# A fused attention and mixture-of-experts kernel: the first expert weight's split moved from the setup into four batches, and the setup's loads and TensorE products put in another order

## The reference

```python
x = x + conv(_ln_c(x))                 # x: 8 x 16 x 16 x 256, "conv" is axial attention
t = _to_tokens(x)                      # 2048 tokens of 256
t = t + ffn(_ln_t(t))                  # 8 experts, one per token, 256 places each

# conv: q, k, v = linear maps of x (256 -> 256)
r_attn = softmax(q . k along a row    - gw * dist(w))
c_attn = softmax(q . k along a column - gw * dist(h))
out = (r_attn v + c_attn v) @ Wo.T + bo

# ffn: logits = x2d @ wg; idx = argmax; a token has a place while its expert has one of 256 free
h  = relu(einsum("ecm,emh->ech", di, w1))     # w1: 8 x 256 x 1024
eo = einsum("ech,ehm->ecm", h, w2)            # w2: 8 x 1024 x 256
out = gate * eo, back at the token's row
```

## Time and profile before

| what | before |
|---|---|
| three executions, us | 206.6, 206.73, 295.39 (median 206.73) |
| span of the profiled execution, first to last instruction, us | 204.0 |
| what lies around the span: median less span, us | 2.7 |
| mean granted TensorE clock in the span | 0.961 |
| PE, DVE, ACT, POOL busy, share of the span | 91%, 72%, 52%, 50% |

### The profile page before, as it was taken

The page is one execution under the profiler, slowest core; times in us unless marked ns, Lnnn a source line. Parts: engine busy times, 40 slices in busy tenths (PEclk is TensorE's granted clock), DMA queues, the critical chain, the costliest instruction groups (busy, mean ns, idle before and its releaser), DMA issues.

```text
span 204.0 us, 4341 instructions
## 1 busy us (share of the span) xinstructions
PE 185.1 (91%) x1404; PEld 176.7 (87%) x1404; DVE 146.6 (72%) x460; ACT 105.4 (52%) x246; POOL 102.8 (50%) x101
## 2 busy tenths in 40 slices
PE   7799399999999985959799999999999999999990
PEld 7699399998798883849789999999999999999980
DVE  0579998898999999776956584866858496465510
ACT  2368367888678644235043927538192653826000
POOL 3327574246456357558400636639183663918351
PEclk9999889999999999676999999999999999999997
DMA  5799750103712211331387639192753909271010
GB/s 186 210 394 346 223 193 0 56 0 72 292 51 83 69 60 53 105 127 51 104 310 240 178 105 345 32 367 79 235 228 113 348 16 345 96 205 42 3 55 33
DMA packets 23294, 30.86 MB, mean 151 GB/s; under 512 B 2559, under 2 KB 20113, under 8 KB 23280
## 3 DMA queue, kind: packets, MB, share of 16 engines
q1 hardware_dynamic: 20704, 25.81, 38.5%
q0 software_dynamic: 1616, 4.02, 5.5%
q10 hardware_dynamic: 960, 0.85, 1.2%
HBM read 22.57 MB, written 8.45 MB: 152 GB/s over the span
## 4 chain that ended last, share of the span: by engine, by line
PE 64%; DVE 22%; issue 5%; DMA 3%; ACT 2%; SPq 1%; POOLq 1%; POOL 1%; DVEq 0%; ACTq 0%
PE banks_v L506 7%; PE banks_v L513 7%; PE banks_v L507 7%; DVE w_low L1143 4%; PE bank_q L513 3%; PE bank_pT L513 3%; PE bank_pT L506 3%; PE bank_pT L507 3%; DMA wg_sb<-in_L_ffn_wg 3%; PE bank_q L506 3%; PE bank_s L513 3%; PE bank_s L506 3%; PE bank_s L507 3%; PE bank_q L507 3%; PE banks_o L580 2%
## 5 line engine op out<-in xcount | busy, mean ns | idle before, releaser
L456 POOL TENSOR_TENSOR w_low<-w_in_sb,w_high 128x1024 fp32r<-128x1024 f32 x16 | 38.4, 2421 | 17.1 <-ACT w_high L826 16.8
L478 POOL DMA_INDIRECT out<-y,goal x16 | 15.7, 979 | 35.5 <-DVE y L1134 29.1
L826 ACT ACTIVATE w_high<-w_in_sb 128x1024 fp32r<-128x1024 f32 x32 | 31.9, 1052 | 1.4 <-DMA w_in_sb<-in_L_ffn_w 1.4
L1143 DVE TENSOR_TENSOR w_low<-w_in_sb,w_high 128x1024 fp32r<-128x1024 f32 x14 | 28.1, 2044 | 4.5 <-ACT w_high L826 4.3
L426 POOL DMA_INDIRECT slots<-row,slot x14 | 14.2, 1016 | 18.1 <-DVE slot L1086 16.1
L870 ACT ACTIVATE h_high<-bank_xT 128x512 fp32r<-128x512 f32 x8 | 4.8, 597 | 28.5 <-PE bank_xT L513 28.5
L644 PE MATMUL bank_xT<-ones_wide 128*128 128x128 f32 x100 | 17.8, 360 | 1.1 <-DVE ones_wide L893 1.1
L580 PE MATMUL banks_o<-v_sb,pT 128*128 128x264 f32 x64 | 18.1, 411 | 0.6 <-DVE logit L1021 0.5
L644 PEld LDWEIGHTS bank_xT<-ones_wide 128*128 128x128 f32 x100 | 17.2, 272 | 1.1 <-DVE ones_wide L893 1.1
L506 PE MATMUL banks_v<-w_high,h_high 128*128 128x256 f32 x64 | 15.9, 287 | 0.0
L507 PE MATMUL banks_v<-w_high,h_low 128*128 128x256 f32 x64 | 15.7, 283 | 0.0
(11 more groups left out here) (200 smaller groups left out, 614.5 us busy)
## 6 DMA issues: line engine op xcount, KB each, us to landing
w_in_sb<-in_L_ffn_w SPq DMA_DIRECT2D x16, 1024.0 KB
slots<-empty SPq DMA_DIRECT2D x1, 2080.0 KB, 13.7
sl<-slots SPq DMA_DIRECT2D x8, 260.0 KB, 3.2
out<-row SPq DMA_DIRECT2D x7, 256.0 KB
sl<-in_x SPq DMA_DIRECT2D x4, 256.0 KB, 6.0
sl<-in_x SPq DMA_DIRECT2D x2, 512.0 KB, 8.8
table_in<-in_tables SPq DMA_DIRECT2D x1, 292.0 KB, 6.3
w_in_sb<-in_L_conv_Wq ACTq DMA_DIRECT2D x1, 256.0 KB, 3.5
```

What stands on the lines that cost most here:

```text
L456: step = nc.gpsimd.tensor_tensor(w2_low[j][:, half, :], w2_in_sb[:, half, :], w2_high[j][:, half, :].bitcast(f32), ALU.subtract)
L478: nc.gpsimd.indirect_dma_start(out_rows, bass.IndirectOffsetOnAxis(ap=goal[j][:, c:c + 1].bitcast(u32), axis=0), y[j][:, c, :], None, boun ...
L826: nc.scalar.activation(high[j][:, half, :], raw[:, half, :], ACT.Copy).then_inc(ready, 1)
L1143: step = nc.vector.tensor_tensor(w1_low[j][:, c, :], w1_in_sb[:, c, :], w1_high[j][:, c, :].bitcast(f32), ALU.subtract)
```

## The change

On the load queues (SP and ACT) bq's load moves from SP to ACT ahead of the identity, wo goes behind the identity; on SP wg goes ahead of the second group of x, the table and the third group of x ahead of the bias columns bv and bo, and the first w1 behind all of x. On TensorE the qbias product goes ahead of the sum over wg (which goes to another PSUM bank), the first transposes of batch 0 ahead of `fold_values`, and `fold_biases` behind `values`. VectorE follows that order: `masks` and `query_low` ahead of `first_norm(2)`, `values_low` ahead of batch 0's `maxima`, and `query_low` ahead of `first_norm(4)`. The first w1's split is cut into four pieces of 128 x 512: at the end of batches 2, 3, 4 and 5 ScalarE writes a high part and GpSimd a low part. The load of the second w1, which needs the buffer, waits on SP for the fourth piece, behind the store of batch 4's rows and ahead of those of batches 5 and 6.

```diff
-        ps_wgsum, ps_qbias, ... = bank_pT[:, 0:E], ...
+        ps_wgsum, ps_qbias, ... = ps_v[:, 1, 0:E], ...
...
 @block.sync
             load_x(0)
-            load_x(1)
...
                 sp.dma_start(wg_sb[:, :, :], wg.rearrange("(c p) e -> p c e", p=P)).then_inc(wg_in, 16)
+                load_x(1)
                 sp.dma_start(wv_sb, matrix(Wv)).then_inc(wv_in, 16)
+                sp.dma_start(table_in[:, :], tables_in).then_inc(const_in, 16)
+                load_x(2)
...
-            sp.dma_start(w1_in_sb[:, :, :], w1_view[0]).then_inc(w1_in, 16)
             for g in range(3, len(X_GROUPS)):
                 load_x(g)
+            sp.dma_start(w1_in_sb[:, :, :], w1_view[0]).then_inc(w1_in, 16)
...
-            sp.wait_ge(w1_split, 1)
+            pairs(sp, 1, B - 4, store_x2)
+            sp.wait_ge(first_w1_low, 2 * DC)
             sp.dma_start(w1_in_sb[:, :, :], w1_view[1]).then_inc(w1_in, 16)
-            pairs(sp, 1, B - 2, store_x2)
+            peeled(B - 3, store_x2)
+            peeled(B - 2, store_x2)
...
 @block.gpsimd
-            pool.wait_ge(w1_high_ready, DC)
-            nc.gpsimd.tensor_tensor(w1_low[0][:, :, :], w1_in_sb[:, :, :], w1_high[0][:, :, :].bitcast(f32), ALU.subtract).then_inc(w1_split, 1)
             first_rstd(4)
...
                 if not second:
                     scatter_rows(k - 1, j)
...
+                if not second and not last_but_one:
+                    first_w1_part_low(k, j)
+
+            def first_w1_part_low(k, j):
+                pool.wait_ge(first_w1_high, 2 * k + j - 1)
+                c, part = bass.ds(k - 1, 1), slice(j * F // 2, (j + 1) * F // 2)
+                nc.gpsimd.tensor_tensor(w1_low[0][:, c, part], w1_in_sb[:, c, part], w1_high[0][:, c, part].bitcast(f32),
+                                        ALU.subtract).then_inc(first_w1_low, 1)
...
 @block.tensor, batch
+                if first:
+                    fold_values()
                 scores(k, j)
...
                 if first:
-                    fold_biases()
                     query(*after(k, j))
                     pe.wait_ge(m_ready, 1)
                 values(k, j)
+                if first:
+                    fold_biases()
...
 @block.scalar, batch
                 if not second:
                     gate_exp(k - 1, j)
+                if not second and not last_but_one:
+                    first_w1_part_high(k, j)
...
-            split_w1(0, 0)
             sweep(act, batch)
...
 @block.vector, setup and batch
             peeled(0, x_low)
...
+            masks()
...
-            masks()
+            peeled(0, query_low)
             first_norm(2)
-            peeled(0, query_low)
             first_norm(3)
...
                     x_low(*after(k, j))
+                if first:
+                    values_low()
                 maxima(k, j)
...
-                if first:
-                    values_low()
                 if first:
+                    query_low(*after(k, j))
                     first_norm(4)
-                    query_low(*after(k, j))
```

More of the change, by code:

```diff
@@ L358, in _ @@
             peeled(1, load_slots)
-            sp.wait_ge(w1_split, 2)
+            sp.wait_ge(w1_split, 1)
             sp.dma_start(w1_in_sb[:, :, :], w1_view[2]).then_inc(w1_in, 16)
@@ L653, in _ @@
             step.then_inc(fold_a, 1)
+            pe.wait_ge(bq_in, 16)
+            for d in range(DC):
+                step = product(ps_qbias[:, d:d + 1], wk_sb, bq_sb[:, :].unsqueeze(2), chunk[d], whole)
+            step.then_inc(qbias_made, 1)
             pe.wait_ge(wg_in, 16)
@@ L664, in _ @@
             step.then_inc(fold_wo, 1)
-            pe.wait_ge(bq_in, 16)
             pe.wait_ge(wgc_ready, 1)
-            for d in range(DC):
-                step = product(ps_qbias[:, d:d + 1], wk_sb, bq_sb[:, :].unsqueeze(2), chunk[d], whole)
-            step.then_inc(qbias_made, 1)
             fold_logits()
@@ L673, in _ @@
             peeled(0, query)
-            fold_values()
             sweep(pe, batch)
@@ L694, in hidden @@
                 e = 2 * k + j
-                pe.wait_ge(w1_split, e + 1)
+                wait(pe, w1_split, e)
+                if isinstance(e, int) and e == 0:
+                    pe.wait_ge(first_w1_low, 2 * DC)
                 pe.wait_ge(gT_ready, e + 1)
```

27 lines of the change are left out of this document (16 added, 11 removed).

## The result

The changed kernel took 213.44 us (median of four, 212.57 to 213.99) against 206.71 for before (median of four): 1.028 times as long, with a 95% interval from 1.022 to 1.034. The forecast of 207.5 and its range, 202.8 to 210.6, are missed. For before I had reckoned 2.7.

What follows compares the result with a forecast made beforehand. It took TensorE's wait for m_low (3.4 us) as the setup's bound and VectorE as the sweep's from batch 3 on. Terms -3.6 + 4.4 = +0.8 us on the 204.0 span, plus 2.7 around it, gave 207.5 us; range 202.8 to 210.6.

Steps and rivals of the forecast that it cites:

- reckoned 2.7: Outside the profiled span: 2.7 us of measured time around the 204.0 us span, added to reach the forecast.
- the setup gain: Setup: m_low no longer waits for GpSimd's split, batch 2 starts near 30.5 and not 34.05; gain 3.6 us.
- since work has only been permuted: Setup up to batch 0's scores: they start near 16.0 as before, so nothing is gained there.
- 0 to 0.5 us late: Setup: the second x group is issued 0.5 us later, so VectorE's norm of it runs 0 to 0.5 us late.
- the late waits of batch 1: Setup: TensorE waits 1.4 us for xn and 0.8 for prob; a clock fall there would lose 1.0 to 1.5 us.
- The sweep's term: VectorE's batches 3 to 6: each GpSimd piece holds VectorE some 1.1 us; cost 4.4 us.
- ScalarE's pieces and SP: Sweep: ScalarE's pieces, 0.55 us each, are covered by 1.7 us; SP's later second w1 load costs nothing.
- The pieces are nearly free: Rival, sweep: VectorE's short instructions slip in before or between the pieces; cost 0.8 us, time 203.9; chance 0.27.
- the first-come rule: Sweep: whichever of VectorE and GpSimd issues first keeps the port pair, so short VectorE instructions would hold GpSimd up.
- Slower, by the clock in the sweep: Rival, sweep: holes in TensorE's batches lower its clock, 1 us in each of four batches; 211.5 us; chance 0.08.
- The setup gains less: Rival, setup: waits are only exchanged and the clock falls; gain 2.2, cost 4.4 to 5.2, 208.9 to 209.7; chance 0.12.
- The split isn't off the setup's path: Rival, setup: something else holds m_low, so nothing is gained; 211 us; chance 0.03.

Runs made afterwards that it cites:

- the quiet spots: Two kernels, e5 and e6: the kernel before with GpSimd's first-w1 subtraction cut into four pieces at other setup places; 204.91 and 204.63 us against 208.71.
- e7: The changed kernel with 14 more warm-up products on TensorE ahead of its wait for Wo; 212.05 us, ratio to before 1.014.
- e8: The changed kernel with GpSimd's piece ahead of the batch's two scatters and not behind them; 208.35 us against 208.71 for before.
- e1: The kernel before with only the first w1's split moved into the sweep, and SP's wait with it; 211.18 us against 207.74 for before.
- e2: The changed kernel with all loads in the old order; 211.09 us, ratio to before 1.017.
- e3: The changed kernel with Wo's load ahead of bq on ACT; 213.05 us, ratio to before 1.030.
- e12: The kernel before with wg's load ahead of the second x group on SP; one run, 207.45 us.
- e5: The kernel before with GpSimd's first-w1 subtraction in four pieces: behind m_ready, behind the xb pair, two behind batch 1's probabilities; 204.91 us against 208.71 for before.
- e13: The changed kernel with wg's load behind the second x group again; 213.35 us, ratio to before 1.031.
- e11: The changed kernel with all loads in the old order and GpSimd's piece ahead of the two scatters; 206.23 us against 208.02 for before.
- e9: The kernel before with one more column load of bq (1 KB) ahead of Wo, into a tile nobody reads; one run, 206.82 us.
- e6: The kernel e5 with six more warm-up products on TensorE ahead of its wait for wg; 204.63 us against 208.71 for before.

## Why the prediction was wrong

**The mechanism of the setup gain was right.** m_low's first instruction went to 0.16 us, and the quiet spots show what that is worth: batch 2 starts 2.5 us earlier, and 3.9 us with the clock kept up (one profile each).

**The step that failed is the sentence that nothing is gained up to batch 0's scores, "since work has only been permuted".** It rested on two landings that I let stand. I let the second x group be "0 to 0.5 us late"; it was 2.8 late. And I never asked for Wo, which the change puts behind bq and the identity, though TensorE's first transposes wait on its semaphore: 3.1 us. The row that I used, wg with 6.5 us, told how long a small load takes, not what it does to the loads behind it. In place of the gain of 3.6 us came a loss of 1.7. By e7, some 1.6 to 2.1 of the 5.3 us between them are the clock, which fell behind the 3.1 us of waiting; why Wo itself landed 3.8 us slower stays open. I had put the clock's fall behind the late waits of batch 1, where it did not come, and priced it at 1.0 to 1.5 us.

**The sum over the profiled execution** closes with this: 5.3 us missed in the setup, 1.8 in the sweep, 0.3 behind it, less the 0.9 by which I had put too much around the span, are the 6.5 us between 207.5 and 213.99. The setup is by far the larger part.

**The sweep's term was mis-sized: 6.2 us for 4.4.** The mechanism was right, and the place too: one instruction of VectorE's choice beside each piece, always shifted. I had taken 1.1 us each, out of 0.7 to 1.3, bounding the hold by the piece's own length. Measured are 1.4 on average (the four slips add to 5.7) and 1.7 at most. Rows 6 and 7 already held the reason: both times VectorE's instruction had started some 0.5 us ahead of GpSimd's row. I had read from them only that GpSimd wins, and not that the hold can reach 0.5 us further back than the piece. 1.3 + 0.5 - 0.16 gives 1.6 us. The other 0.5 us comes in batch 7, where VectorE waited for TensorE at 0.52 of its clock, a term that the sum put at nothing.

**ScalarE's pieces and SP** cost nothing, as forecast: the piece takes 0.61 us, and with the same ScalarE pieces and the same SP wait e8's stretch is 67.97 us against 67.90. The second w1 was issued at 87.65 and no wait for it shows.

**The rivals.** "The pieces are nearly free" is what e8 made of it, by another mechanism than the first-come rule: they are free beside VectorE instructions with an operand in PSUM. "Slower, by the clock in the sweep" had a time near the result (211.5) and is the smaller part of the cause: some 0.1 us in batch 4 and 0.5 in batch 7 and not 1 us in each of four batches, and over the whole stretch the granted clock was 0.91 against 0.92 in before. "The setup gains less" came nearer with 208.9 to 209.7 and lacked the landings. "The split isn't off the setup's path" is out: no wait for m_low is left.

The Trainium skill (SBUF — State Buffer, section "Who interferes with whom") says that a VectorE instruction with two SBUF inputs contends with a GpSimd instruction that reads SBUF, and that whichever issues first keeps the port pair. Its first half is borne out on both sides here: shifted (two SBUF operands) is held up to 1.85 us, xT_low (one in PSUM) never beyond its 0.69. Its second half is not decided: shifted's row starts first and is held, which contradicts it if the rows' starts are the issues, and agrees if GpSimd holds the ports already 0.5 us ahead of that row, where its scatter still runs.

## What to carry to other kernels

A helper instruction on GpSimd costs or doesn't by what VectorE does beside it. With all its operands in SBUF VectorE stops until it ends (5.6 to 6.2 us for four pieces here), and not only with two of them: the copy of rows 6 and prob read one SBUF tensor each. With an operand in PSUM it doesn't stop (0.1 us for the same four), nor do the statistics. So look for the stretch of VectorE's order that reads PSUM, and anchor the piece there with a wait.

When loads change places, follow each load to its first reader, the big ones behind the small too, and take the landing from a row of a load that stood in such a place. Where none stood there, the landing is an unknown (3.8 us for Wo here) and belongs in the range. Look also at what a wait counts: here transposes that needed only the identity waited for Wo, because the two share a semaphore.

Before reordering a whole setup for one conflict, try to move the one instruction that conflicts.

## What the runs showed of the hardware

- Behind a scatter, GpSimd's hold on VectorE begins up to 0.5 us ahead of its next instruction's recorded start: shifted 48.11 against w_low 48.63, copy 78.00 against xb 78.47. Both had time to finish ahead of GpSimd's start, and neither did. w_low at 101.64, against 102.17, two instructions of a 128x1024 half each, took until GpSimd's end at 106.92 and then 2.2 us more, so it too had got next to nowhere before. In all three a scatter on GpSimd ends where its next row starts, and in e8 a copy (56.62, 0.34 us for 0.15) was held to the end of a scatter with nothing behind it, so the hold may belong to the scatter's end. Ahead of a GpSimd row that stands behind no scatter it doesn't show: in before, chosen at 47.47 took its 0.17 us against rstd at 47.63.
- Held beside GpSimd were VectorE instructions with two SBUF operands (m_low 4.04 us for 0.16, shifted 1.85 for 0.16) and with one (copy 1.80 for 0.15, prob 1.60 for 0.61 a pair, minus_mean 0.62 for 0.17). Not held were those with an operand in PSUM (xT_low 0.69, s_col 0.41) and the statistics (1.40 a group of four).
- Waits of TensorE of 1.3 to 4.2 us in the setup, and the granted clock from 11.4 to 18.1 us behind them: 0.52 in after (3.1 us), 0.56 in e1 (2.3; 0.52 from 12.5 to 19.3), 0.51 in e2 (2.1), 0.50 in e3 (4.2) and e12 (1.9), but 0.75 in e5 with the same 2.1, in e13 (1.7) and in e11 (1.3), and 1.00 in e9 with the same 1.3. Filling the wait (e7, e6) kept it at 1.00. So the wait's length alone doesn't tell how long the clock stays down, or whether it falls.
- One unchanged kernel moves by 1.3% between executions on one chip: before took 205.77 to 208.44 us beside e11 in twelve of thirteen executions, with mean granted clocks from 0.942 to 0.974. So of these edits, those of 1 to 2 us show in the stretches of a trace and hardly in the medians.
